# Wide attention scored in pairs of heads, each on its own 64 rows of TensorE, with a third score buffer and a ring of two banks

## What is computed

```
qkv = x @ W_qkv + b_qkv                       # x: 1024 x 256 per batch
scores = einsum('bqhi,bkhi->bhqk', Q, K) / sqrt(64)
scores = scores + mask                        # -10000 above the diagonal
probs = softmax(scores, axis=-1)
vals = einsum('bkhi,bhqk->bqhi', V, probs)
return vals @ W_out + b_out
```

## Time and profile before

| | |
|---|---|
| median of 3 runs | 5967.7 us (5962.17 to 5971.76) |
| the profiled execution | 5970.14 us |
| its span, first to last instruction | 5968.3 us |
| TensorE busy | 76% of the span |
| VectorE busy | 69% |
| ScalarE busy | 46% |
| GpSimd busy | 32% |
| mean granted TensorE clock | 0.862 |

### The profile page before, as it was taken

The page is one execution under the profiler, slowest core; times in us unless marked ns, Lnnn a source line. Parts: engine busy times, 40 slices in busy tenths (PEclk is TensorE's granted clock), DMA queues, the critical chain, the costliest instruction groups (busy, mean ns, idle before and its releaser), DMA issues. The chain is left out here.

```text
span 5968.3 us, 83328 instructions
## 1 busy us (share of the span) xinstructions
PE 4526.2 (76%) x30341; PEld 2886.9 (48%) x30341; DVE 4103.4 (69%) x8455; ACT 2762.3 (46%) x6047; POOL 1903.4 (32%) x1563
## 2 busy tenths in 40 slices
PE   4444578988677778888777678989777686999776
PEld 2333345656434454666533454656533453666334
DVE  5999957877786757778787656877788555222630
ACT  2334324666253633666345451666445360554333
POOL 2555512444322521443333430434333331000001
PEclk7666689999787889999888788999988798999888
DMA  3000001000201120000221121000031101000312
GB/s 123 11 11 25 1 22 25 18 13 15 52 17 71 45 90 21 14 15 10 48 32 63 42 65 58 13 13 13 15 62 37 62 28 49 17 10 10 63 62 72
DMA packets 113333, 213.59 MB, mean 36 GB/s; under 512 B 25728, under 2 KB 70632, under 8 KB 109552
## 3 DMA queue, kind: packets, MB, share of 16 engines
q1 hardware_dynamic: 104736, 190.94, 11.7%
q0 software_dynamic: 6144, 16.79, 0.9%
q10 hardware_dynamic: 2048, 0.53, 0.0%
HBM read 154.38 MB, written 49.73 MB: 34 GB/s over the span
## 5 line engine op out<-in xcount | busy, mean ns | idle before, releaser
L1492 DVE MAX8 vals<-work 128x8 f32<-128x128 f32 (+7 forms) x1536 | 1080.2, 743 | 0.4
L1866 POOL TENSOR_SCALAR keep<-ssb,vals 128x128 bf16<-128x128 f32 (+7 forms) x512 | 875.3, 1721 | 0.0
L469 PE MATMUL ring<-ident,pr 128*128 128x128 f32 x2304 | 475.9, 325 | 436.8 <-POOL pr L1871 361.4
L1853 POOL TENSOR_TENSOR pool_step<-ones 128x2 f32<-128x2 f32 x256 | 49.6, 194 | 2325.8 <-DVE vals L1492 2317.2
L1506 DVE MATCH_REPLACE8 work<-vals,work 128x128 f32<-128x128 f32 (+7 forms) x1024 | 750.8, 739 | 0.0
L576 PE MATMUL pA<-SC 128*128 128x512 f32 (+3 forms) x1536 | 623.5, 515 | 105.7 <-ACT SC L1204 53.4
L1871 POOL TENSOR_TENSOR pr<-keep,pr 128x128 f32<-128x128 bf16 (+7 forms) x512 | 647.1, 1284 | 1.2 <-ACT pr L1137 1.2
L469 PEld LDWEIGHTS ring<-ident,pr 128*128 128x128 f32 x2304 | 320.3, 165 | 602.4 <-POOL pr L1871 386.5
L1492 DVE MAX8 vals<-ssb 128x8 f32<-128x128 f32 (+7 forms) x512 | 363.0, 750 | 331.2 <-ACT ssb L1131 315.3
L1621 DVE TENSOR_REDUCE nmax<-pA 128x1 f32<-128x1024 f32 (+7 forms) x512 | 384.6, 751 | 297.3 <-PE pA L577 286.3
L1143 ACT ACTIVATE prT<-ring 128x512 f32<-128x512 f32 (+1 forms) x768 | 382.1, 500 | 419.9 <-PE ring L469 418.2
(11 more groups left out here) (225 smaller groups left out, 8263.9 us busy)
## 6 DMA issues: line engine op xcount, KB each, us to landing
SC<-in_w SPq DMA_DIRECT2D x64, 512.0 KB, 7.0
stage<-parts SPq DMA_DIRECT2D x384, 64.0 KB, 2.4
parts<-SC SPq DMA_DIRECT2D x72, 256.0 KB, 4.2
SC<-parts SPq DMA_DIRECT2D x144, 128.0 KB, 7.7
SC<-in_wqkv SPq DMA_DIRECT2D x32, 384.0 KB, 3.0
rows_out<-SC SPq DMA_DIRECT2D x92, 128.0 KB, 1.7
SC<-rows_in SPq DMA_DIRECT2D x20, 512.0 KB, 3.9
SC<-in_ffn_we SPq DMA_DIRECT2D x4, 2048.0 KB, 10.1
```

Source lines behind the costliest of these rows:

```text
L469: mm = pe.transpose(r[:, blk % 4 * P:blk % 4 * P + P], pr0[:, p % 2, blk * P:blk * P + P], ident[:, :])
L1492: m = v.max(vals0[:, y, i, 8 * n:8 * n + 8], src[:, lo:hi])
L1866: pool.tensor_scalar(keep0[:, lo:hi], ssb0[:, p % 2, lo:hi], vals0[:, p % 2, i, TOPK - 1:TOPK], None, ALU.is_ge).then_inc(s["k"], 1)
```

## The change

Queries are copied once, for both heads, to `qT`. The scores are made for a pair of units at a time: each head's matmul contracts over its own 64 rows only, and the matmuls of the two heads alternate piece by piece; both masks follow at the end of the pair. The scores have three buffers of two banks now, used by turns: `pA[1]`, `pA[0]` and a new one, `pC`, which is `pV` together with the third bank of the ring. So while the wide attention runs, the ring has two banks. The order of the loops on TensorE and ScalarE goes by pairs, the values of pair p-1 come before the second transposes of pair p, and the ticks of both units come at the end of a pair on these two engines. VectorE's order stays. The memset of `qm` and its semaphore go.

The diff, with unchanged context cut:

```diff
@@ -209,8 +209,11 @@
         pA = [ps(f"pA{i}", [P, N]) for i in range(2)]
-        pV = ps("pV", [P, 512])
-        ring = [ps(f"ring{i}", [P, 512]) for i in range(3)]
+        pC = ps("pC", [P, N])
+        pV = pC[:, 0:512]
+        ring = [ps(f"ring{i}", [P, 512]) for i in range(2)] + [pC[:, 512:N]]
+        wide_s = [pC, pA[1], pA[0]]
         rows_y = [pA[0][:, 0:D], pA[1][:, 0:D]]
@@ -312,7 +315,7 @@
         prT = cut(0, 4096).rearrange("p (a n) -> p a n", n=N)
-        qm = cut(4096, 2048).rearrange("p (j n) -> p j n", j=2)
+        qT = cut(4096, N)
         kT = cut(6144, N)
@@ -360,7 +363,6 @@
         s_out = sem("s_out")
-        s_qz = sem("s_qz")
         s_rf = sem("ring_filled")
@@ -379,18 +381,25 @@
         N_CONST = 23
-        place = {}
+        place, lies = {}, []
         block = ctx.enter_context(nc.Block())
         @block.tensor
         def _(pe):
+            banks = [3]
+            last = [-1, -1, -1]
             def bank(key):
                 n = place[key] = len(place)
-                if n >= 3:
-                    pe.wait_ge(s_re, n - 2)
-                return ring[n % 3]
+                i = min(range(banks[0]), key=lambda i: last[i])
+                if last[i] >= 0:
+                    pe.wait_ge(s_re, last[i] + 1)
+                last[i] = n
+                lies.append(i)
+                return ring[i]
             def emptied(key):
@@ -565,16 +574,21 @@
                 s = a1
-                def scores(G, u):
-                    i, j = WD.unit(u)
+                def scores(G, p):
+                    i, _ = WD.unit(2 * p)
                     w = (i + 1) * P
-                    if u >= 2:
-                        pe.wait_ge(s["e"], G * 16 + u - 1)
-                    p = pA[(u + 1) % 2]
+                    if p:
+                        pe.wait_ge(s["e"], G * 16 + 2 * p - 1)
                     for lo in range(0, w, 512):
                         hi = min(lo + 512, w)
-                        pe.matmul(p[:, lo:hi], qm[:, j, i * P:i * P + P], kT[:, lo:hi], start=True, stop=(hi < w))
-                    pe.matmul(p[:, w - P:w], identm[:, :], tri[:, 1, :], start=False, stop=True).then_inc(s["s"], 1)
+                        for u in (2 * p, 2 * p + 1):
+                            rows = slice(u % 2 * 64, u % 2 * 64 + 64)
+                            pe.matmul(wide_s[u % 3][:, lo:hi], qT[rows, i * P:i * P + P], kT[rows, lo:hi],
+                                      start=True, stop=(hi < w))
+                    for u in (2 * p, 2 * p + 1):
+                        pe.matmul(wide_s[u % 3][:, w - P:w], identm[:, :], tri[:, 1, :], start=False,
+                                  stop=True).then_inc(s["s"], 1)
                 def turn(G, u):
@@ -610,6 +624,8 @@
                 emptied(("n2", b, 3))
+                banks[0] = 2
+                pe.wait_ge(s_re, last[2] + 1)
                 for g in range(8):
@@ -625,26 +641,28 @@
                     at("wide", g * 17)
-                    pe.wait_ge(s["eqk"], G * 3 + 2)
+                    pe.wait_ge(s["eqk"], G * 2 + 1)
                     for t in range(NT):
                         for k in range(KC):
                             mm = pe.matmul(pA[0][:, t * P:t * P + P], hT[:, k, t * P:t * P + P],
                                            wq[:, k, 2 * P:3 * P], start=(k == 0), stop=(k == KC - 1))
                     mm.then_inc(s["pj"], 1)
-                    pe.wait_ge(s["eqk"], G * 3 + 3)
+                    pe.wait_ge(s["eqk"], G * 2 + 2)
                     scores(G, 0)
                     pe.wait_ge(s["ev"], G + 1)
-                    scores(G, 1)
-                    for u in range(16):
-                        if u + 2 < 16:
-                            scores(G, u + 2)
-                        turn(G, u)
-                        if u % 2 and u >= 3:
-                            values(G, u // 2 - 1)
-                        at("wide", g * 17 + 1 + u)
+                    for p in range(8):
+                        if p + 1 < 8:
+                            scores(G, p + 1)
+                        turn(G, 2 * p)
+                        if p:
+                            values(G, p - 1)
+                        turn(G, 2 * p + 1)
+                        for u in (2 * p, 2 * p + 1):
+                            at("wide", g * 17 + 1 + u)
                 values(b * 8 + 7, 7)
                 spread(b * 8 + 7)
                 pe.wait_ge(s["nm"], b * 8 + 8)
+                banks[0] = 3
             def flip(b, at):
@@ -957,7 +975,7 @@
                         sp.wait_ge(a1["ev"], G + 1)
-                        sp.wait_ge(a1["eqk"], G * 3 + 3)
+                        sp.wait_ge(a1["eqk"], G * 2 + 2)
                         group_weights(g + 1)
@@ -1078,7 +1096,7 @@
                 act.wait_ge(s_rf, n + 1)
-                return ring[n % 3]
+                return ring[lies[n]]
             act.wait_ge(s_mld, 48)
@@ -1201,7 +1219,7 @@
                     act.wait_ge(s["mx"], G * 16 + u + 1)
-                    act.activation(pr[:, u % 2, 0:w], pA[(u + 1) % 2][:, 0:w], ACT.Exp,
+                    act.activation(pr[:, u % 2, 0:w], wide_s[u % 3][:, 0:w], ACT.Exp,
                                    bias=nmax[:, u % 4:u % 4 + 1],
@@ -1212,17 +1230,14 @@
                         act.activation(prT[:, u % 4, c * 512:c * 512 + w], r[:, 0:w], ACT.Copy).then_inc(s_re, 1)
-                act.wait_ge(s_qz, b + 1)
+                act.wait_ge(pj[0]["dr"], min(b + 2, B) * 192)
                 for g in range(8):
                     G = b * 8 + g
                     act.wait_ge(s["w"], (G + 1) * 48)
                     act.mul(bq_s[:, :], bqk_sb[:, 0:1], 0.125).then_inc(s["bs"], 1)
                     act.wait_ge(s["bs"], G + 1)
                     act.wait_ge(s["pj"], G * 3 + 1)
-                    for j in range(2):
-                        rows = slice(j * 64, j * 64 + 64)
-                        act.activation(qm[rows, j, :], pA[0][rows, :], ACT.Identity, scale=0.125,
-                                       bias=bq_s[rows, :]).then_inc(s["eqk"], 1)
+                    act.activation(qT, pA[0][:, :], ACT.Identity, scale=0.125, bias=bq_s[:, :]).then_inc(s["eqk"], 1)
                     act.wait_ge(s["pj"], G * 3 + 2)
@@ -1230,13 +1245,16 @@
                     exponential(G, 0)
-                    for u in range(16):
-                        if u + 1 < 16:
-                            exponential(G, u + 1)
-                        turned(G, u)
-                        if u % 2 and u >= 3:
-                            out_of_psum(G, u // 2 - 1)
-                        at("wide", g * 17 + 1 + u)
+                    for p in range(8):
+                        exponential(G, 2 * p + 1)
+                        turned(G, 2 * p)
+                        if p:
+                            out_of_psum(G, p - 1)
+                        if p + 1 < 8:
+                            exponential(G, 2 * p + 2)
+                        turned(G, 2 * p + 1)
+                        for u in (2 * p, 2 * p + 1):
+                            at("wide", g * 17 + 1 + u)
                 out_of_psum(b * 8 + 7, 7)
@@ -1618,7 +1636,7 @@
                         v.wait_ge(s["e"], G * 16 + u - 3)
-                    v.tensor_reduce(nmax[:, u % 4:u % 4 + 1], pA[(u + 1) % 2][:, 0:w], AX, ALU.max,
+                    v.tensor_reduce(nmax[:, u % 4:u % 4 + 1], wide_s[u % 3][:, 0:w], AX, ALU.max,
                                     negate=True).then_inc(s["mx"], 1)
@@ -1636,10 +1654,14 @@
                     rowmax(G, 1)
-                    for u in range(16):
-                        if u + 2 < 16:
-                            rowmax(G, u + 2)
-                        at("wide", g * 17 + 1 + u)
+                    for p in range(8):
+                        if p + 1 < 8:
+                            rowmax(G, 2 * p + 2)
+                            at("wide", g * 17 + 1 + 2 * p)
+                            rowmax(G, 2 * p + 3)
+                            at("wide", g * 17 + 2 + 2 * p)
+                        else:
+                            at("wide", g * 17 + 2 + 2 * p)
                 inverse(b * 8 + 7)
@@ -1953,9 +1975,6 @@
                 norm("n1", b)
-                pool.wait_ge(pj[0]["dr"], min(b + 2, B) * 192)
-                pool.wait_ge(s_x, b * 16 + 16)
-                pool.memset(qm, 0.0).then_inc(s_qz, 1)
                 norm("n2", b)
```

## The result

The changed kernel takes 6181.2 us (median of 4 runs, 6171.3 to 6188.9) against 5965.2 us: 1.036 times the time, 95% interval 1.0343 to 1.0376. The profiled execution took 6171.3 us, 201 more than that of before. It is slower, as forecast (6073, range 5930 to 6235), by about twice the forecast step (216 us against 105).

The account below looks back on a forecast made before the run. It took TensorE's queue as the bound before and a longer TensorE-ScalarE chain after: +33 us in batch 3 and +72 in company, +105 on 5970.1, gives 6075, or 6073 for the median; range 5930 to 6235.

Parts of the forecast that it names:

- a longer chain on TensorE and ScalarE: Wide attention: next scores wait behind values, their copy and an exponential; +4.2 us a group alone, +3 in company.
- The signs that I had named: Wide attention: checks on the trace, among them 54 to 55 us a group alone and 71 to 75 in company.
- The round for tile 7: Group alone, scoring tile 7, turning 6, values of 4: one round of the chain takes 7.0 us, against 6.5 before.
- The wait for a bank: In that round: values reuse the bank of the turn's first chunk and wait 0.54 us, plus a 0.17 change of shape.
- 24.5 slots: Score matmuls of a group: partial overlap of the two heads cuts 36 slots of 0.43 us, saving 4.9 us.
- the clock is not the issue: Wide attention, in company and alone: granted clock 0.98 and 0.99, the 2.4 GHz level, so no clock term.
- I let these two cancel: In company: ticks filling TensorE's wait for the exponential offset their banks' waits for ScalarE, leaving +3 us a group.
- Rival 4: Batches 0 to 2: the ring of two hurts in company, +8 us a group, total 6193 us; 10%.
- Rival 1: Batches 0 to 2: top-k work fills the gaps, TensorE stays the bound, -2.2 us a group, total 5948; 15%.
- Rival 3: Score matmuls: disjoint rows do not run together, the chain grows another 4.9 us in all 32 groups, 6230; 12%.
- Rival 2: Score matmuls: full overlap and free changes of shape shorten the chain, total near 5835 us; 4%.
- the small edits: Memset removed, queries copied once, odd units' scores issued early to free VectorE: each counted as nothing.

Follow-up runs that it names:

- exp_first: The changed kernel with ScalarE taking the exponential of the next pair's first unit ahead of the copy of the previous pair's values; 6122.2 us.
- rows_only: The kernel of before with each score matmul over the head's own 64 rows, unit by unit, queries copied once, no memset; 6229.1 us.
- filled: The changed kernel with four full-row bf16 matmuls, results overwritten, ahead of TensorE's wait for each pair's exponential; 6159.3 us.
- ring_two: The kernel of before with its ring cut from three to two banks in the wide attention and nothing else changed; 6181.7 us.
- ticks_apart: The changed kernel with the top-k's ticks again after each unit on TensorE and ScalarE, not clumped at the pair's end; 6143.1 us.
- full_rows: The changed kernel with zero-masked queries and 128-row score matmuls back; order, score buffers and ring of two kept; 6292.9 us.

## Why the prediction was right, and where it was off

**The direction: right, in the main by luck.** I expected a longer chain on TensorE and ScalarE in all four batches. What made the kernel slower was the ring of two in company, which I had set at nothing on balance, and alone a fallen clock, which I had ruled out. The signs that I had named show it: a group alone was to take 54 to 55 us and takes 52.5, and in company 71 to 75 and takes 77.6.

**The chain alone: there, but no longer than before.** The round for tile 7 came as described, with the waits at the two places named (L1231 before the values, L1222 before the scores), and exp_first, which cuts it, gives 2.7 us a group back. But it takes 6.2 us where I had 7.0, and the kernel before took 6.5. The scores with masks and changes took 2.0 us (5455.27 to 5457.26), and I had put them at 2.35 and two changes of 0.17, 2.7 in all; this is 0.7 of the 0.8 us. The wait for a bank with the change of shape before the values was 0.66, as good as my 0.54 and 0.17. The rounds that end with tiles 7, 3 and 1 came out shorter than forecast as well, 5.4, 6.0 and 5.6 us against 6.3, 6.9 and 6.4.

**The scores: wrong between the bounds.** I counted 24.5 slots for a group from the in-order A, A, B, B. The rows of a pair with two whole pieces show 4 slots and not 5, and at that rate a group has 18, the bound of perfect overlap. The Trainium skill ("TensorEngine Tiling (Array Packing)", Theoretical Speedup), up to 2x, was the better guide: the trace agrees, with both heads' passes 0.01 us apart and 0.43 us between later passes. The Trainium skill's rule of a drain at a change of mode (same title, Key Properties) fits too, but is small: the mask follows the last pass by 0.52 us and not 0.43, and in rows_only a change costs 0.07 us at most, under the 0.17 I took.

**The clock: missed.** That "the clock is not the issue" held for the kernel before only. Alone the change lowers it to 0.94, which filled prices at 2.3 us a group. That filled in for the overstated chain: I had +4.2 alone, without the clock's fall it is about -0.4 (50.2 in filled less 50.6), measured is +1.9. So the seven groups of batch 3 brought +13 us and its whole stage +17, where I had +33.

**In company: the term that was mis-sized.** It is "I let these two cancel", with the chain's +3 a group put on top. Measured is +8.5 over the three batches. The failed half is that the ticks' banks wait for ScalarE: I set it against the filling of TensorE's gaps and called it even, while the three waits of the table above grew from 6.7 to 72.8 us in batch 1. I had priced the ring only where the values wait for one copy on TensorE's chain. That price was fair alone (2.4 us a group in ring_two), and in company the ring costs 7.7. It also limits how far TensorE may run ahead of ScalarE. ScalarE in turn waits for row maxima that VectorE makes between steps of the top-k; that this passes through the ring to TensorE is my reading, and no run isolates it. Rival 4, "The ring of two hurts in company, +8 a group", 6193 us, is what came nearest (ring_two: +7.7), and I gave it 10%. But 4.8 of its 8 us were clumps of ticks, 0.6 us at each of eight pairs. The clumps were worth only 2.2 to 2.5 us a group (ticks_apart), and ring_two, which has none, loses 7.7, split about evenly between the wide attention's own fills and the ticks. So its figure is partly luck too.

**The other rivals.** Rival 1 (TensorE stays the bound in company) is out: TensorE is busy for 432 of 543 us there, against 431 of 483. Rival 3 (rows don't run together) is out by the timeline and by full_rows. Rival 2 had its premises, full overlap and nearly free changes, and still did not come about: the ring, which it priced at 2.5 us a group in company, cost 7.7, and the pair order cost 4.0 on top. Of the small edits, the single copy of the queries, the memset and VectorE's idle time show nothing against my zeros; they had no run of their own.

## What to carry to other kernels

Before taking a bank from a ring that several streams share in order, count who fills it between two of the producer's other duties. Here the third bank was worth 211 us and a fourth 24, and a run with nothing but the smaller ring gives the price before anything else is written. Work saved on the leading engine pays only as far as the in-order partner can follow: place the instruction that releases the next round ahead of copies nobody waits for (59 us here), and keep interleaved work spread out (38 us). If a change halves the rows of the matmuls, read the granted clock again afterwards.

## What the hardware showed that I had not expected

- Two heads' fp32 passes on rows 0 to 63 and 64 to 127 start within 0.01 us of each other and run side by side, into different PSUM banks: 0.43 us for both where one took 0.43.
- Matmuls over 64 rows bring the granted clock down although TensorE is busy: 0.87 at 98% busy (rows_only) against 0.99 at 96% with 128 rows. Groups took 52.9 us at the 2.4 GHz level and up to 67.1 with stretches at 1.2 GHz, one of them 30.7 us long with TensorE busy throughout.
- Four full-row bf16 matmuls (some 0.4 us) put into each wait brought the clock of the changed kernel alone from 0.94 to 1.00 and the group from 52.5 to 50.2 us.
